# The setup of a Perceiver kernel in a new order: keys, queries, mask and weights

## The reference

```python
x = x + _L0_xattn_ref(_layernorm(x), ctx_2048, itok, W_kvc, W_dq, W_uq, W_qr, W_uk, W_kr, W_uv, W_o)

def _L0_xattn_ref(q, kv, seg_id, ...):      # x: 16 x 64 rows of 256; kv: 16 x 1601 rows of 256
    kv_c = kv @ W_kvc                       # 64 columns
    q_c = q @ W_dq                          # 96 columns
    q_nope = (q_c @ W_uq)                   # 16 heads of 128
    q_rope = _rope(q_c @ W_qr)              # 16 heads of 64
    k_nope = (kv_c @ W_uk)
    k_rope = _rope(kv_c @ W_kr)
    v = (kv_c @ W_uv)
    scores = (q_nope @ k_nope + q_rope @ k_rope) / sqrt(192)
    good = (k_ids <= seg_id) & (k_ids >= seg_id - 8)
    attn = softmax(where(good, scores, -1e30))
    return (attn @ v) @ W_o
x = x + _L0_attn_ref(_layernorm(x), ...)    # 16 heads of 16, 64 tokens
x = x + _L0_ffn_ref(_layernorm(x), ...)     # top 2 of 8 experts and 2 shared ones
```

## Time and profile before

| | |
|---|---|
| median of 3 runs | 517.2 us (516.69 to 518.62) |
| the profiled execution | 517.89 us, of which the span shown is 516.1 us |
| PE (matmul) busy | 499.9 us, 97% |
| VectorE busy | 249.5 us, 48% |
| ScalarE busy | 185.1 us, 36% |
| GpSimd busy | 60.1 us, 12% |
| mean granted TensorE clock | 0.992 |

### The profile page before, as it was taken

The page is one execution under the profiler, slowest core; times in us unless marked ns, Lnnn a source line. Parts: engine busy times, 40 slices in busy tenths (PEclk is TensorE's granted clock), DMA queues, the critical chain, the costliest instruction groups (busy, mean ns, idle before and its releaser), DMA issues.

```text
span 516.1 us, 10576 instructions
## 1 busy us (share of the span) xinstructions
PE 499.9 (97%) x3878; PEld 363.7 (70%) x3878; DVE 249.5 (48%) x549; ACT 185.1 (36%) x534; POOL 60.1 (12%) x71
## 2 busy tenths in 40 slices
PE   8799999999999999998999998999999999999997
PEld 7476777777877788886788885555555555556886
DVE  2565876876766668888562221212222222222234
ACT  2157567566566444444411111212212112111110
POOL 2000000000000122132006500000000000000750
PEclk9799999999999999999999999999999999999999
DMA  8700000000991009400613162787877878852331
GB/s 296 314 22 1 20 22 3 17 20 19 353 418 46 2 18 412 185 0 1 241 69 133 71 243 67 271 281 264 320 271 269 322 261 280 316 186 81 93 111 41
DMA packets 24455, 82.05 MB, mean 159 GB/s; under 512 B 2880, under 2 KB 16512, under 8 KB 20320
## 3 DMA queue, kind: packets, MB, share of 16 engines
q1 hardware_dynamic: 21536, 75.93, 40.2%
q0 software_dynamic: 1536, 4.20, 2.5%
q10 hardware_dynamic: 1344, 1.38, 0.8%
HBM read 73.10 MB, written 8.39 MB: 158 GB/s over the span
## 4 chain that ended last, share of the span: by engine, by line
PE 86%; DVE 6%; issue 3%; ACT 2%; DMA 2%; another core or an unknown queue 1%; SPq 1%; POOL 0%; DVEq 0%; ACTq 0%; POOLq 0%
PE ps L1813 17%; PE ps L1317 12%; PE ps L1721 12%; PE ps L1837 9%; PE ps L1733 6%; PE ps L1396 5%; PE ps L1346 5%; PE ps L1365 5%; PE ps L1488 3%; PE ps L1384 3%; DMA w_routed<-in_ctxT 2%; PE ps L1338 1%; ACT w_routed L1096 1%; PE ps L1498 1%; PE ps L1677 1%
## 5 line engine op out<-in xcount | busy, mean ns | idle before, releaser
L1813 PE MATMUL ps<-w_routed,xnT 128*64 x320 | 93.8, 436 | 1.6 <-DVE x_sb L967 1.6
L1721 PE MATMUL ps<-xT_all,w_shared 128*128 128x256 f32 x320 | 75.7, 380 | 0.0
L1813 PEld LDWEIGHTS ps<-w_routed,xnT 128*64 128x64 f32 x320 | 42.0, 137 | 38.4 <-issue 27.2
L1721 PEld LDWEIGHTS ps<-xT_all,w_shared 128*128 128x128 f32 x320 | 60.3, 190 | 8.4 <-issue 0.4
L1096 ACT ACTIVATE w_routed<-ps,neg_top 128x128 f32<-128x128 f32 x128 | 45.1, 379 | 15.3 <-DVE neg_top L637 15.3
L1317 PEld LDWEIGHTS ps<-consts_a,w_routed 128*128 128x128 f32 x336 | 38.6, 145 | 13.5 <-issue 10.4
L1837 PE MATMUL ps<-w_routed,hidT 128*64 x200 | 47.4, 384 | 0.0
L1317 PE MATMUL ps<-consts_a,w_routed 128*128 128x128 f32 x336 | 45.9, 282 | 1.1 <-DVE w_routed L829 0.5
L1813 PE MATMUL ps<-x_up,xnT 128*64 128x384 f32 (+1 forms) x160 | 46.9, 436 | 0.0
L1813 PE MATMUL ps<-w_shared,xnT 128*64 128x384 f32 (+1 forms) x160 | 46.9, 436 | 0.0
L1259 ACT ACTIVATE sil<-ps 128x256 f32<-128x256 f32 x40 | 15.3, 384 | 85.1 <-PE ps L1721 60.9
(11 more groups left out here) (181 smaller groups left out, 870.8 us busy)
## 6 DMA issues: line engine op xcount, KB each, us to landing
w_routed<-in_w_routed SPq DMA_DIRECT2D x8, 1920.0 KB, 14.3
x_up<-in_w_routed SPq DMA_DIRECT2D x10, 1280.0 KB, 5.8
w_shared<-in_w_routed SPq DMA_DIRECT2D x10, 1280.0 KB, 5.9
b_down<-in_w_routed SPq DMA_DIRECT2D x10, 640.0 KB
w_shared<-in_w_routed SPq DMA_DIRECT2D x10, 640.0 KB, 4.9
w_shared<-in_w_shared SPq DMA_DIRECT2D x1, 3840.0 KB, 11.8
w_shared<-in_w_uvo SPq DMA_DIRECT2D x1, 2560.0 KB, 15.2
x_slots<-sil SPq DMA_DIRECT2D x16, 160.0 KB, 2.2
```

The source lines that it names most:

```text
L1721: last = pe.matmul(ps[:, UP_BANK[m], half_ * D:(half_ + 1) * D].rearrange("p (n t) -> p n t", n=2), w_shared[:, j, at:at + P], xT_all[:, i ...
L1813: last = pe.matmul(ps[rows, b, 0:hi - lo], xnT[:, k, rows], w, start=k == 0, stop=k == KT - 1)
```

## The change

The setup is put in another order.

- SP issues the weights of the key fold ahead of those of the query fold, and `w_qr` after the context of tile 0.
- TensorE folds the keys first, then the queries; then it does `xT`, `kv`, `qc`, `y_rope`, `y_lat` (before: `xT`, `qc`, `kv`, `y_lat`, `y_rope`). `kv` no longer waits for the folded queries. PSUM banks change with it.
- VectorE copies the compressed query of tile 0 (before: ScalarE).
- The mask's three passes move from VectorE to GpSimd, behind a new semaphore `seg_moved`.
- Four transfers are issued later: x of tiles 2 to 7 by ScalarE after the key copies, `w_uvo` by ScalarE after `lat_out`; `consts_b` and `a_w` by SP after the branch and after the context of tile 1, which now goes ahead of them.

```diff
@@ SP
-            sp.dma_start(w_shared[:]...[:, 0:H * (QC + KVC)], dram["w_uqk"]).then_inc(wu_in, 16)
             sp.dma_start(w_kT[:], dram["w_kT"]).then_inc(wk_in, 16)
             sp.dma_start(w_kd[:], dram["w_kd"]).then_inc(wk_in, 16)
-            sp.dma_start(w_q[:, 1], dram["w_qr"]).then_inc(wr_q_in, 16)
+            sp.dma_start(w_shared[:]...[:, 0:H * (QC + KVC)], dram["w_uqk"]).then_inc(wu_in, 16)
...
             load_ctx(0)
-            sp.dma_start(w_shared[:]...[:, H * (QC + KVC):H * (QC + 2 * KVC + D)], dram["w_uvo"]).then_inc(wv_in, 16)
-            sp.dma_start(consts_b[:], dram["consts_b"]).then_inc(moe_in, 16)
-            sp.dma_start(w_routed[:, E // 4, 0:4 * KT * D], dram["a_w"]).then_inc(aw_in, 16)
+            sp.dma_start(w_q[:, 1], dram["w_qr"]).then_inc(wr_q_in, 16)
...
             general(sp, g_tile, g_first)
-            with sp.Fori(1, NT) as i:
+            load_ctx(1)
+            sp.dma_start(consts_b[:], dram["consts_b"]).then_inc(moe_in, 16)
+            sp.dma_start(w_routed[:, E // 4, 0:4 * KT * D], dram["a_w"]).then_inc(aw_in, 16)
+            with sp.Fori(2, NT) as i:
                 load_ctx(i)
@@ GpSimd
             for i in range(2):
                 rstd_of(i, i + 1)
+            pool.wait_ge(const_in, 16)
+            pool.wait_ge(seg_moved, 1)
+            link(pool.tensor_tensor(dist, keypos..., seg..., ALU.subtract))
+            link(pool.tensor_tensor(dist, dist, dist, ALU.mult))
+            pool.tensor_scalar(win[:], dist, (LOOKBACK / 2) ** 2, -NEG, ALU.is_gt, ALU.mult).then_inc(win_ready, 1)
@@ VectorE
-            link(dve.tensor_scalar(seg[:], seg[:], -LOOKBACK / 2, None, ALU.add))
-            link(dve.tensor_tensor(dist, keypos..., seg..., ALU.subtract))
-            link(dve.tensor_tensor(dist, dist, dist, ALU.mult))
-            dve.tensor_scalar(win[:], dist, (LOOKBACK / 2) ** 2, -NEG, ALU.is_gt, ALU.mult).then_inc(win_ready, 1)
+            dve.tensor_scalar(seg[:], seg[:], -LOOKBACK / 2, None, ALU.add).then_inc(seg_moved, 1)
+
+            query_compressed(0)
             dve.wait_ge(flag_ps, 1)
@@ ScalarE
-            act.dma_start(x_sb[:, 2:, :], x_tiles[:, 2:, :]).then_inc(x_in, 16)
...
             xT_out(0)
-            qc_out(0)
             kv_raw_out(0)
+            act.dma_start(x_sb[:, 2:, :], x_tiles[:, 2:, :]).then_inc(x_in, 16)
             lat_out(0)
+            act.dma_start(w_shared[:]...[:, H * (QC + KVC):H * (QC + 2 * KVC + D)], dram["w_uvo"]).then_inc(wv_in, 16)
```

More of the change, by code:

```diff
@@ L497, in _ @@
                 rstd_of(i, i + 1)
+            pool.wait_ge(const_in, 16)
+            pool.wait_ge(seg_moved, 1)
+            link(pool.tensor_tensor(dist, keypos[:].unsqueeze(1).to_broadcast([P, NT, P]),
+                                    seg[:].unsqueeze(2).to_broadcast([P, NT, P]), ALU.subtract))
+            link(pool.tensor_tensor(dist, dist, dist, ALU.mult))
+            pool.tensor_scalar(win[:], dist, (LOOKBACK / 2) ** 2, -NEG, ALU.is_gt, ALU.mult).then_inc(win_ready, 1)
             def g_tile(i):
@@ L711, in _ @@
             normed(0, 1, xn, xT_ps, xn_ready, 0)
-            dve.wait_ge(const_in, 16)
             dve.wait_ge(seg_in, 16)
@@ L1030, in _ @@
             act.dma_start(seg_i[:], dram["seg"]).then_inc(seg_in, 16)
-            act.dma_start(x_sb[:, 2:, :], x_tiles[:, 2:, :]).then_inc(x_in, 16)
             def two(b):
                 return ps[:, b:b + 2, :].rearrange("p b (h t) -> p (b h) t", t=P)
-            act.wait_ge(absorb_q_ps, 1)
-            act.copy(w_q[:, 0].rearrange("p h c -> p (h c)"), ps[0:QC, 2:4, :].rearrange("p b n -> p (b n)")).then_inc(absorb_q, 1)
             act.wait_ge(absorb_k_ps, 1)
             act.copy(w_k[:, :, KVC:], ps[:, 6, 0:KT * R].rearrange("p (k r) -> p k r", r=R)).then_inc(absorb_k, 1)
+            act.wait_ge(absorb_q_ps, 1)
+            act.copy(w_q[:, 0].rearrange("p h c -> p (h c)"), ps[0:QC, 4:6, :].rearrange("p b n -> p (b n)")).then_inc(absorb_q, 1)
             def lat_at():
@@ L1058, in xT_out @@
                 act.copy(xnT[:], ps[:, 0, 0:D].rearrange("p (k t) -> p k t", t=P)).then_inc(xT_done, 1)
-            def qc_out(i):
-                act.wait_ge(qc_ps, i + 1)
-                act.copy(qcT[:], ps[0:QC, 1, 0:P]).then_inc(qc_done, 1)
             def kv_raw_out(i):
@@ L1170, in _ @@
             xT_out(0)
-            qc_out(0)
             kv_raw_out(0)
+            act.dma_start(x_sb[:, 2:, :], x_tiles[:, 2:, :]).then_inc(x_in, 16)
             lat_out(0)
+            act.dma_start(w_shared[:].rearrange("p e n -> p (e n)")[:, H * (QC + KVC):H * (QC + 2 * KVC + D)], dram["w_uvo"]
+                          ).then_inc(wv_in, 16)
             def g_tile(i):
@@ L1587, in _ @@
             keep_warm(WARM_UP)
-            pe.wait_ge(wu_in, 16)
-            for h in range(H):
-                last = pe.matmul(ps[0:QC, 2 + h // 8, (h % 8) * KVC:(h % 8 + 1) * KVC], w_uq[:, h, :], w_uk[:, h, :],
-                                 start=True, stop=True)
-            last.then_inc(absorb_q_ps, 1)
             pe.wait_ge(wk_in, 16 * 2)
@@ L1596, in _ @@
             last.then_inc(absorb_k_ps, 1)
+            pe.wait_ge(wu_in, 16)
+            for h in range(H):
+                last = pe.matmul(ps[0:QC, 4 + h // 8, (h % 8) * KVC:(h % 8 + 1) * KVC], w_uq[:, h, :], w_uk[:, h, :],
+                                 start=True, stop=True)
+            last.then_inc(absorb_q_ps, 1)
             pe.wait_ge(const_in, 16)
             xT(0)
+            pe.wait_ge(absorb_k, 1)
+            kv(0)
             qc(0)
             pe.wait_ge(flag_set, 1)
-            pe.matmul(ps[0:1, 5, 0:1], half[:, 0:1], far_n[:], start=True, stop=True).then_inc(flag_ps, 1)
-            pe.wait_ge(absorb_k, 1)
-            pe.wait_ge(absorb_q, 1)
-            kv(0)
-            y_lat(0)
+            pe.matmul(ps[0:1, 7, 0:1], half[:, 0:1], far_n[:], start=True, stop=True).then_inc(flag_ps, 1)
             pe.wait_ge(wr_q_in, 16)
             y_rope(0)
+            pe.wait_ge(absorb_q, 1)
+            y_lat(0)
             def g_tile(i):
```

12 lines of the change are left out of this document (4 added, 8 removed).

## The result

| | before | the change |
|---|---|---|
| median, 22 executions each | 518.61 us (516.64 to 521.33) | 516.86 us (514.58 to 522.62) |
| ratio to before | | 0.9966, 95% interval 0.995 to 0.9982 |
| the profiled execution | 517.89 us, span 516.1 | 515.22 us, span 513.4 |
| mean granted clock in it | 0.992 | 1.0 |

So the kernel gains 0.34%, some 1.8 us, which lies within the 0.5% that the prediction counts as no change. The profiled execution alone gains 2.67.

A forecast was written before the change was run, and what follows sets the result against it. TensorE, fully busy once tiles run, bounds the kernel, so only earlier first scores gain: 23.9 us, 3.0 earlier, less 0.3 for low clock, gives 2.7 off the median 517.2, 514.5 us; range 512.7 to 517.3.

The forecast's parts named there:

- The gain comes from an earlier start of the first scores, one to one: First scores matmul, 26.97 us before: the time it starts earlier carries through the tiles behind almost one to one.
- w_uqk lands at 8.5 (bounds 7.7 and 8.8): Query fold's weights: landing at 8.5 instead of 6.84 us, queued behind 304 KB of key weights.
- Fold order ... 11.35: Folds on TensorE: the key fold fits in the wait, and the query fold of 2.85 us ends at 11.35.
- The rotation's own 3.67 us and the move of y_rope ahead: VectorE's rotation after the rotary y, now first: still 3.67 us, queries rotated at 19.3 instead of 22.94.
- this edit alone would give 3.6 us: Rotary half of y first on TensorE: worth 3.6 us by itself, 2.3 if the low clock stays.
- TensorE's branch over by 18.5: Branch over TensorE's general path: starts at 14.8, fetches code in 1.2 us, ends at 18.5; 21.0 with a loaded fetch.
- So the stall goes from TensorE's branch to VectorE's and ScalarE's: Ahead of VectorE's copy of query transposes: code fetches for both engines' branches end at 22.0, putting scores at 23.9.
- Low clock, 0.3 us: Near the first scores: 0.3 us charged for remaining low clock, whose full price is about 1.6.
- Mask and later weights: Mask on GpSimd, 5.7 us, worth nothing, slowing VectorE's passes beside it at most 60%; later w_uvo hidden, 5 us spare.
- Loaded fetches: Rival, chance 0.32: VectorE's and ScalarE's code takes 3.7 us, scores at 25.0 to 26.6, gain 0.3 to 1.9, 516.0.
- Nothing left of the wait: Rival, chance 0.18: code fetches of 1.2 us and full clock, scores at 22.4 to 22.6, gain 4.4, 512.8.
- Fetch behind w_uvo: Rival, chance 0.06: code waits behind w_uvo's pieces until 28, VectorE's copy starts 3.5 us later than before, 520.7.

The follow-up runs named there:

- experiment 3, last: The change with the w_uqk transfer first in SP's queue again, TensorE still folding keys first: 515.65 us, 0.9969.
- the third timing of the change: The change itself with no edit, timed again beside the filled kernel on the same chip: 518.8 us, 0.9992.
- the best version: The change with the fold order undone and ScalarE copying key fold, x transpose, then query fold: 513.49 us, 0.9925; again 513.6 us, 0.9905.
- experiment 4: The runs of the best version, against the kernel before: 513.49 us, 0.9925, and again 513.6 us, 0.9905.
- the version with both parts: The kernel before with the four later transfers held back and the rotary half of y first, fold order as before: 515.98 us, 0.9951.
- the filled kernel: The change with five more warm-up matmuls on TensorE between the key fold and the query fold: 517.54 us, 0.9979.

## Why the prediction was right or wrong

The time, 516.86 us, lies in the range of 512.7 to 517.3 and 2.4 above the 514.5 forecast. Against its own 518.61 the change gained 1.8 us of the 2.7 forecast, and nothing that can be told from zero in the two later measurements. The forecast's chain was only partly right: one step failed outright, the fold order had the wrong sign, two terms were mis-sized, and one cost was not in the sum.

**The gain comes from an earlier start of the first scores, one to one: right.** 2.22 us earlier there, 2.67 at the last matmul, 2.67 in the profiled execution.

**"w_uqk lands at 8.5 (bounds 7.7 and 8.8)": mis-sized.** It landed at 10.1. I let it queue behind the 304 KB of key weights alone. The transfers of after and then of before, from issue to landing, show what else went ahead:

```profile
w_shared<-in_w_uqk SPq DMA_DIRECT2D x1, 1280.0 KB, 8.1
...
consts_a<-in_consts_a ACTq DMA_DIRECT2D x1, 320.0 KB, 3.8
x_sb<-in_x ACTq DMA_DIRECT2D x1, 256.0 KB, 3.2
```

```profile
consts_a<-in_consts_a ACTq DMA_DIRECT2D x1, 320.0 KB, 8.1
x_sb<-in_x ACTq DMA_DIRECT2D x1, 256.0 KB, 6.9
```

ScalarE's two transfers, 576 KB, used to land after `w_uqk` and now land before it. As an estimate, 304 + 576 = 880 KB at the 277 GB/s of 7 to 12 us are 3.2 us; the delay was 10.13 - 6.84 = 3.3. It is not the same in every execution: in the two later profiles of the change `w_uqk` landed at 10.5 and 11.0, in the kernel without TensorE's branch at 9.0. With `w_uqk` issued first (experiment 3, last) these two take 7.0 and 7.8 us again. Everything behind moved by this: y started at 15.54 instead of 13.7, the queries were rotated at 21.2 instead of 19.3.

**"Fold order ... 11.35" as a harmless step: wrong in sign.** I counted the key fold as filling the wait. The order costs 1.4 us in the profiles (24.75 - 23.37) and some 2 us in the ratios (0.9922 without it, 0.9966 with it, on different chips). Beside the third timing of the change, on one chip, the best version lay 5.2 us lower.

**The rotation's own 3.67 us and the move of y_rope ahead: right.** From the first pass (17.53) to the end of the add (21.20) it took 3.67. But "this edit alone would give 3.6 us" was wrong: alone it gave 0.1 at the scores and 0.4 at the key transpose, for the branch ended 0.2 us behind the rotation. It needed both.

**"TensorE's branch over by 18.5": mis-sized, and the other bound, 21.0, was nearer.** It started at 16.5, its packet was sent 2 us later and not 1.2, and it was over at 21.3. I took little to be under way. But ScalarE had issued the rest of x (768 KB) at 14.23 and it landed 4.9 us later, right across the fetch; with x early the packet came after 0.9 us. The Trainium skill, page "Runtime: NRT & Kernel Launch", section "Instruction fetch mechanics", calls such a taken branch a fetch stall without a price; here it cost 3.39 to 6.37 us in the kernels run.

**"So the stall goes from TensorE's branch to VectorE's and ScalarE's": failed.** No such stall exists. Their branches take 67 and 54 ns, before and after; the earlier trace rows already said so, with 67 ns at 22.6. I took the 8 KB packet 1.2 us later for one that the branch waited for, though the engine's next work did not wait for it. VectorE's copy started at 22.86, 1.08 behind the first query transpose, as the sum had it for the transposes alone. From the copy to the scores it was 1.89 us, as worked out (1.92). The error hid the other two: the false stall added 1.6 us (22.0 instead of 20.4), and the late weights and branch took 1.9 and more. That 23.9 came near 24.75 is luck.

**Low clock, 0.3 us: not in the sum as it came.** I looked for it behind the hole at 20 us only. The new hole at 8 to 11 us is one place where it now falls, in some executions and not in others. That fits a median that gained 1.8 while the profiled execution, which had no low clock in the setup, gained 2.7.

**Mask and later weights: right for the change, both nothing** for the time as such. The mask's last pass with its bf16 output took GpSimd 3.65 us, not 1.9, and ended at 15.5, still 9 us early. But "60% more" for VectorE's passes beside it was far too little where they met: with the fold order undone one took 1.73 us instead of 0.27 (experiment 4). In the change GpSimd's first two passes were over before VectorE's began. Holding the weights back cost the fold of `w_uvo` nothing and helped the branch.

**The rivals.** "Loaded fetches" had the load right (2.0 and 3.7 us for TensorE's packet) on the wrong engines. "Nothing left of the wait" came close only with the old fold order. "Fetch behind w_uvo" had nothing to act on, as the two engines' branches wait for no code; its 0.85 us for a piece is 16.1 / 21 = 0.77 by the earlier trace rows, and no row gives its 21.3, but neither decides anything. The rule of the Trainium skill, page "DMA: Bandwidth & Descriptors", section "Queues, rings and completion order", on packets from one ring was not tested by it.

## What to carry to other kernels
Before a wait is moved, list every chain that ends at the same place, with its end time: here shortening one of two that ended 0.2 us apart moved the next step by 0.4 or 1.2 us, both together by 2.2. Put first on an engine the work whose data lands first and that is long enough to cover the next landing, and count all queues' bytes, not just the own queue's, for when that is. A code packet near a branch need not be a stall; read the branch's own duration, and read the clock of several executions before a profile's gain is believed. Work that moves to a free engine can still slow the busy one, so look at what runs beside it in the new order and not in the old.

## What the runs showed of the hardware
- The wait of a taken branch depends on what the DMA engines carry: 3.39 us with x early (its packet 0.9 us after the start; 69 GB/s moved in 16.5 to 18.5 us), 4.83 in the change (2.0 us; 364 GB/s), 6.37 in the kernel before (3.7 us; 362 GB/s). So the rate alone doesn't set it; what does, beside it, isn't shown. Some 1.4 to 1.6 us pass between the end of the packet and the end of the branch in each. Only TensorE paid it; the other engines' branches over their own slow paths took 45 to 67 ns.
- One program ran with a mean granted clock from 0.983 to 1.0 from execution to execution (514.47 to 522.62 us). With the wait for the fold weights filled it was 0.992 to 1.0. The length of one wait does not tell it alone: behind 2.81 us ahead of the key transpose, in the version with both parts, the transposes ran at 2.4 GHz (1.91 us for 16), behind 1.95 us in the filled kernel partly at 1.2 GHz (2.71).
- VectorE's passes over 128 x 128 float32 took 0.27 to 0.29 us alone and 1.68 to 1.87 beside a GpSimd pass over 128 x 1024 with SBUF inputs, in three profiles. Why it was one pass in each, and not all that met GpSimd, isn't shown.
- GpSimd took 1.90 us for a pass over 128 x 1024 float32 and 3.65 where it wrote bf16:

```profile
9.88 1.89 POOL L503 TENSOR_TENSOR xT_all<-xT_all 128x1024 f32<-128x1024 f32 x1
11.87 3.65 POOL L504 TENSOR_SCALAR w_routed<-xT_all 128x1024 bf16<-128x1024 f32 x1
```

These two rows also differ in their operation, so what part the output type has isn't shown.
